# Graph layers on one core: first-stage transfers on other queues, carry index from rows on chip, ninth parts turned two by two

## What is computed

```python
h = relu(layer_norm(x))
# layer 0, per edge and head
score = exp(clip(sum(k[src] * q[dst]) / 8, -5, 5))
wv = segment_sum(v[src] * score, dst) / (segment_sum(score, dst) + 1)
g = h @ Wf + bf + wv @ Wo + bo
x = x + g + layer_norm(g) * gamma + beta
h = relu(layer_norm(x))
# layer 1, per edge; sh: 9 numbers per edge
k = mlp2(edge, k_w1, ...) * sum_s(sh[:, s] * (h[src] @ Cqk[:, s, :]))
v = mlp2(edge, v_w1, ...) * sum_s(sh[:, s] * (h[src] @ Cv[:, s, :]))
alpha = segment_softmax(sum(q[dst] * k), dst)
return x + batch_norm(h @ Wself + segment_sum(v * alpha, dst) @ Wout)
```

## Time and profile before

| | us |
|---|---|
| Median of 3 runs | 3783.44 (3783.2 to 3785.74) |
| Profiled execution: its own time | 3787.59 |
| Profiled execution: span, first to last instruction | 3785.8 |
| First stage, to 182 us | 182 |
| Edge stage of layer 0, to 1254 us | 1072 |
| Between the edge stages, to 1428 us | 174 |
| Edge stage of layer 1, to 3650 us | 2222 |
| Closing stage | 136 |

### The profile page before, as it was taken

The page is one execution under the profiler, slowest core; times in us unless marked ns, Lnnn a source line. Parts: engine busy times, 40 slices in busy tenths (PEclk is TensorE's granted clock), DMA queues, the critical chain, the costliest instruction groups (busy, mean ns, idle before and its releaser), DMA issues. The chain is left out here.

```text
span 3785.8 us, 86852 instructions
## 1 busy us (share of the span) xinstructions
PE 3367.5 (89%) x26344; PEld 3215.3 (85%) x26344; DVE 2836.6 (75%) x4894; ACT 1252.2 (33%) x3131; POOL 1977.1 (52%) x2000
## 2 busy tenths in 40 slices
PE   2099999999999327999999999999999999999963
PEld 1088888888888227999999999999999999999953
DVE  4266666666666227899999999999999989999953
ACT  1033333333333113333333334333333433333320
POOL 3377777777777335544444444444444444444430
PEclk8599999999999658999999999999999999999975
DMA  6499999999999213444444444444444444444420
GB/s 232 164 264 280 279 279 279 280 281 279 278 280 277 85 46 102 122 127 129 126 122 129 129 122 125 130 127 122 128 129 123 125 130 128 121 128 130 123 83 31
DMA packets 845629, 622.17 MB, mean 164 GB/s; under 512 B 492271, under 2 KB 734643, under 8 KB 845292
## 3 DMA queue, kind: packets, MB, share of 16 engines
q1 hardware_dynamic: 681454, 502.39, 43.9%
q0 software_dynamic: 56640, 87.65, 9.8%
q10 hardware_dynamic: 107478, 31.50, 3.7%
HBM read 335.87 MB, written 286.31 MB: 164 GB/s over the span
## 5 line engine op out<-in xcount | busy, mean ns | idle before, releaser
L1410 ACT ACTIVATE z_hi<-bank 128x512 fp32r<-128x512 f32 (+1 forms) x1010 | 559.2, 595 | 1095.8 <-PE bank L1341 1095.7
L803 POOL DMA_INDIRECT kv<-kv_tab,src_i x808 | 762.4, 944 | 284.8 <-issue 189.1
L1315 POOL DMA_INDIRECT xg<-h_tab,src_i x808 | 785.7, 972 | 221.6 <-issue 188.6
L1325 POOL TENSOR_TENSOR kq<-kvs,q_of 128x512 f32<-128x512 f32 x202 | 259.7, 1286 | 951.3 <-DVE kvs L1487 951.3
L1366 PE MATMUL bank<-C_hi,z_hi 128*128 128x256 f32 x4040 | 679.5, 299 | 0.0
L1477 DVE TENSOR_TENSOR z_lo<-bank,z_hi 128x512 fp32r<-128x512 f32 x808 | 520.9, 686 | 190.6 <-ACT z_hi L1410 190.0
L1366 PE MATMUL bank<-C_lo,z_hi 128*128 128x256 f32 x4040 | 609.7, 281 | 0.0
L1341 PE MATMUL bank<-ident,z 128*128 128x128 f32 x4040 | 542.4, 273 | 62.4 <-DVE z L1462 62.4
L1462 DVE TENSOR_TENSOR z<-xg,sh 128x1152 f32<-128x1152 f32 x404 | 549.5, 1360 | 9.2 <-DMA xg<-h_tab,src_i 9.2
L1366 PEld LDWEIGHTS bank<-C_hi,z_hi 128*128 128x128 f32 x4040 | 534.7, 190 | 1.1
L1366 PEld LDWEIGHTS bank<-C_lo,z_hi 128*128 128x128 f32 x4040 | 533.3, 188 | 0.0
(11 more groups left out here) (242 smaller groups left out, 4386.4 us busy)
## 6 DMA issues: line engine op xcount, KB each, us to landing
w_tab<-wsb SPq DMA_DIRECT2D x202, 512.0 KB, 3.4
win<-w_tab SPq DMA_DIRECT2D x202, 512.0 KB, 3.5
sum_edge<-rowt SPq DMA_DIRECT2D x202, 288.0 KB, 2.5
q_edge<-zq SPq DMA_DIRECT2D x202, 256.0 KB
qs<-q_edge SPq DMA_DIRECT2D x202, 256.0 KB, 2.8
sum_edge<-rows ACTq DMA_DIRECT2D x202, 136.0 KB
qs<-q_edge SPq DMA_DIRECT2D x202, 128.0 KB
drow<-dst_tab SPq DMA_DIRECT2D x202, 128.0 KB, 3.2
```

The lines of the kernel that those rows point to most:

```text
L803: pool.indirect_dma_start(kv[b][:, q, :], None, kv0_tab, bass.IndirectOffsetOnAxis(ap=src_i[:, i * Q + q:i * Q + q + 1], axis=0))\
L1315: pool.indirect_dma_start(xg[b][:, q, :], None, h1_tab, bass.IndirectOffsetOnAxis(ap=src_i[:, i * Q + q:i * Q + q + 1], axis=0))\
L1325: pool.tensor_tensor(kq[:, :].rearrange("p (q o) -> p q o", q=Q), kvs[b][:, :, 0:O1], q_of[b % 2][:, :].rearrange("p (q o) -> p q o", q=Q) ...
L1410: nc.scalar.activation(z_hi[b % 2][f, k, :], bank[ZB[k]][f, :], ACT.Copy).then_inc(hi_out, 1)
```

## The change

In the first block SyncE issues the four fills after its three loads, and ACT the pads, the two `near` loads, and then all 31 weights, 25 of which stood in the third block. In the third block SyncE's queue holds the 28 fills and, after them, the first queries; ACT issues the rows first, the two table pads after its copies of `lastrow`, and after its last copy of `kvq` the node tables, the 16-bit list and the mask. The side loads are gone: DVE makes the carry index for 808 tiles on one partition from the turned rows `dst_e` and `lastrow`, PE turns it by seven transposes, DVE copies it. Between the edge stages POOL's scatter waits for the group of four tiles that it needs next. In the edge stage of layer 1, z keeps eight parts a tile; the ninth parts of four tiles lie together in `z_last`, made by one DVE instruction, and PE turns two tiles' ninth parts as one, so the fifth part is two transposes; ACT's copy and DVE's remainder of it become two instructions each, of 64 partitions and two tiles.

```diff
-        sp.wait_ge(pad_set, 4)
...
+        sp.wait_ge(pad_set, 1)
+        for k in range(4):
+            sp.dma_start(*fills[k]).then_inc(filled[k], 16)
 
     @block.scalar
     def _(act):
-        act.wait_ge(pad_set, 1)
-        for k in range(4):
-            act.dma_start(*fills[k]).then_inc(filled[k], 16)
+        act.wait_ge(pad_set, 3)
+        act.dma_start(dst_flat[E:EP + P].unsqueeze(0), padi[:, :]).then_inc(lin, 16)
+        act.dma_start(src_flat[E:EP].unsqueeze(0), zrow[0:1, :, :].bitcast(I32).rearrange(
+            "p a d -> p (a d)")[:, 0:EP - E]).then_inc(lin, 16)
+        act.wait_ge(lin, 64)
+        for n in range(2):
+            act.dma_start(near[:, n, :], dst_flat[n:n + P * NTE].rearrange("(p e) -> p e", p=P))\
+               .then_inc(near_in, 16)
         act.wait_ge(w2z, 3)
         for a, b in loads0:
             act.dma_start(a, b).then_inc(w0_in, 16)
+        for a, b in loads:
+            act.dma_start(a, b).then_inc(W_SEM, 16)
...
         for k in range(4, len(fills)):
             sp.wait_ge(filled[k % 4], 16 * (k // 4))
             sp.dma_start(*fills[k]).then_inc(filled[k % 4], 16)
-            if k == 7:
-                for a, b in loads:
-                    sp.dma_start(a, b).then_inc(W_SEM, 16)
-                for g in range(7):
-                    n = P if g < 6 else NT - 6 * P
-                    lo = 1 if g == 0 else 0
-                    sp.dma_start(before_r[lo:n, g, :], dst_tab[g * P + lo - 1:g * P + n - 1, P - 1:P],
-                                 allow_slow_non_contiguous=True).then_inc(sides_in, 16)
-                    sp.dma_start(after_r[0:n, g, :], dst_tab[g * P + 1:g * P + n + 1, 0:1],
-                                 allow_slow_non_contiguous=True).then_inc(sides_in, 16)
-                sp.wait_ge(dst16_set, 2)
...
-            if k == FILL_BEFORE:
-                sp.wait_ge(proj_out, len(pj_groups))
...
         sp.wait_ge(tabs, 64)
 
         sp.wait_ge(first_got, 16 * 7)
...
-        sp.wait_ge(mask_set, 2)
...
         sp.wait_ge(first_put, 16 * 7)
         sp.wait_ge(dst16_out, 32)
         sp.wait_ge(mask_out, 32)
...
+        for rows, tab in ((dst_r, dst_tab), (src_r, src_tab)):
+            act.dma_start(rows[:, 0:6, :], tab[0:6 * P, :].rearrange("(g t) p -> t g p", g=6))\
+               .then_inc(rows_in, 16)
+            act.dma_start(rows[0:NT - 6 * P, 6, :], tab[6 * P:NT, :]).then_inc(rows_in, 16)
...
+        act.dma_start(q0_tab[N:N + 1, :], zrow[0:1, 0, :]).then_inc(tabs, 16)
+        act.dma_start(q1_tab[N:N + 1, :], zrow[0:1, 0:2, :].rearrange("p a d -> p (a d)")).then_inc(tabs, 16)
...
+        act.wait_ge(proj_out, len(pj_groups))
+        act.dma_start(kv0_tab.rearrange("(p j) d -> p j d", j=NJ), kvq[:, :, 0:2 * D]).then_inc(tabs, 16)
+        act.dma_start(q0_tab[0:N, :].rearrange("(p j) d -> p j d", j=NJ), kvq[:, :, 2 * D:3 * D]).then_inc(tabs, 16)
...
+        act.wait_ge(dst16_set, 2)
...
+        act.wait_ge(mask_set, 2)
...
+        first, final = dst_e[0:1, :], lastrow[0:1, :]
+        step(dve.memset(into[:, 0, 0:1], 0.0))
+        step(dve.tensor_tensor(into[:, 0, 1:], final[:, 0:NTR - 1], first[:, 1:NTR], ALU.is_equal))
+        step(dve.tensor_tensor(into[:, 1, :], first[:, 1:NTR + 1], first[:, 0:NTR], ALU.not_equal))
+        step(dve.tensor_tensor(into[:, 0, :], into[:, 0, :], into[:, 1, :], ALU.mult))
+        step(dve.tensor_scalar(into[:, 0, :], into[:, 0, :], -4.0 * N, 4.0 * N, ALU.mult, ALU.add))
+        dve.tensor_tensor(into[:, 2, :], into[:, 0, :], first[:, 0:NTR], ALU.add).then_inc(into_ready, 1)
...
+        dve.wait_ge(into_mm, 1)
+        step(dve.tensor_copy(into_i[:, 0:6], bank[0][:, 0:6]))
+        step(dve.tensor_copy(into_i[0:NTR - 6 * P, 6:7], bank[0][0:NTR - 6 * P, 6:7]))
...
+        pe.wait_ge(into_ready, 1)
+        for g in range(7):
+            n = P if g < 6 else NTR - 6 * P
+            ins = nc.tensor.transpose(bank[0][0:n, g:g + 1], into[0:1, 2, g * P:g * P + n], ident[0:1, 0:1])
+        ins.then_inc(into_mm, 1)
...
-        pool.wait_ge(q_out, len(groups4))
         for j in range(NJ):
+            if j % 4 == 0:
+                pool.wait_ge(q_out, j // 4 + 1)
...
-z = [sb(f"z{b}", [P, Q, S * D], F32, ph) for b in range(2)]
+z = [sb(f"z{b}", [P, Q, (S - 1) * D], F32, ph) for b in range(2)]
+z_last = [sb(f"z_last{b}", [P, Q * D], F32, ph) for b in range(2)]
...
+def of_half(rows_ap, r):
+    return rows_ap.rearrange("p (h r e) -> p h r e", r=2, e=P)[:, :, r, :]
...
-                for q in range(Q):
-                    ins = nc.tensor.transpose(bank[ZB[k]][:, q * P:(q + 1) * P],
-                                              z[b % 2][:, q, COLS[k]], ident[:, :])
+                turned = [z[b % 2][:, q, k * P:(k + 1) * P] for q in range(Q)] if k < 4 else \
+                    [z_last[b % 2][:, 2 * h * D:2 * (h + 1) * D] for h in range(Q // 2)]
+                for q, part in enumerate(turned):
+                    ins = nc.tensor.transpose(bank[ZB[k]][:, q * P:(q + 1) * P], part, ident[:, :])
...
-                f = slice(D, 2 * D) if k == 4 else slice(0, P)
-                nc.scalar.activation(z_hi[b % 2][f, k, :], bank[ZB[k]][f, :], ACT.Copy).then_inc(hi_out, 1)
+                if k < 4:
+                    nc.scalar.activation(z_hi[b % 2][:, k, :], bank[ZB[k]][:, :], ACT.Copy).then_inc(hi_out, 1)
+                    return
+                for r in range(2):
+                    f = slice(r * D, (r + 1) * D)
+                    ins = nc.scalar.activation(of_half(z_hi[b % 2][f, 4, :], r),
+                                               bank[ZB[4]][f, 0:2 * P].rearrange("p (h e) -> p h e", e=P), ACT.Copy)
+                ins.then_inc(hi_out, 1)
...
+                if half == 0:
+                    dve.tensor_tensor(z_last[b % 2][:, :].rearrange("p (q d) -> p q d", d=D), xg[b][:, :, :],
+                                      sh[b][:, :, S - 1:S].broadcast_to([P, Q, D]), ALU.mult)
                 dve.tensor_tensor(z[b % 2][:, tiles, :].rearrange("p q (s d) -> p q s d", d=D),
-                                  bcast(xg[b][:, tiles, :], 2, S), bcast(sh[b][:, tiles, :], 3, D),
+                                  bcast(xg[b][:, tiles, :], 2, S - 1), bcast(sh[b][:, tiles, 0:S - 1], 3, D),
...
-                    dve.tensor_tensor(z_hi[b % 2][0:D, 4, :], bank[ZB[4]][D:2 * D, :],
-                                      z_hi[b % 2][D:2 * D, 4, :].bitcast(F32), ALU.subtract).then_inc(lo_out, 1)
+                    for r in range(2):
+                        f, g = slice(r * D, (r + 1) * D), slice((1 - r) * D, (2 - r) * D)
+                        ins = dve.tensor_tensor(of_half(z_hi[b % 2][g, 4, :], r),
+                                                bank[ZB[4]][f, 0:2 * P].rearrange("p (h e) -> p h e", e=P),
+                                                of_half(z_hi[b % 2][f, 4, :], r).bitcast(F32), ALU.subtract)
+                    ins.then_inc(lo_out, 1)
```

More of the change, by code:

```diff
@@ L258, in gnn @@
             q0_fill = q0_edge.rearrange("(a p n) d -> a p n d", p=P, n=101)
-            FILL_BEFORE = 17
             fill_parts = [(0, 26), (26, 51), (51, 76), (76, 101)]
@@ L521, in _ @@
                 def _(sp):
[L522 to L525, removed]
                     for k in range(4, len(fills)):
@@ L593, in _ @@
                                              bank[6 + g % 2][0:NP, 0:(b - a) * 3 * D], ACT.Copy).then_inc(proj_out, 1)
+                    act.wait_ge(proj_out, len(pj_groups))
+                    act.dma_start(kv0_tab.rearrange("(p j) d -> p j d", j=NJ), kvq[:, :, 0:2 * D]).then_inc(tabs, 16)
+                    act.dma_start(q0_tab[0:N, :].rearrange("(p j) d -> p j d", j=NJ), kvq[:, :, 2 * D:3 * D]).then_inc(tabs, 16)
+                    act.wait_ge(dst16_set, 2)
+                    act.dma_start(dst16_tab[0:6 * P, :].rearrange("(g t) p -> t g p", g=6), dst16_r[:, 0:6, :])\
+                       .then_inc(dst16_out, 16)
+                    act.dma_start(dst16_tab[6 * P:NT, :], dst16_r[0:NT - 6 * P, 6, :]).then_inc(dst16_out, 16)
+                    act.wait_ge(mask_set, 2)
+                    act.dma_start(mask_tab[0:6 * P, :].rearrange("(g t) p -> t g p", g=6), mask_r[:, 0:6, :])\
+                       .then_inc(mask_out, 16)
+                    act.dma_start(mask_tab[6 * P:NT, :], mask_r[0:NT - 6 * P, 6, :]).then_inc(mask_out, 16)
                     act.wait_ge(W_SEM, n_weights)
@@ L670, in _ @@
                     step(dve.tensor_tensor(over[:, :], tf[:, 0, :], has[:, :], ALU.mult))
-                    dve.wait_ge(sides_in, 16 * 14)
-                    for n, g0, g1 in ((P, 0, 6), (NT - 6 * P, 6, 7)):
-                        at = (slice(0, n), slice(g0, g1))
-                        step(dve.tensor_tensor(into[0:n, 0, g0:g1], before_r[0:n, g0:g1, 0], first_i[at], ALU.is_equal))
-                        step(dve.tensor_tensor(into[0:n, 1, g0:g1], after_r[0:n, g0:g1, 0], first_i[at], ALU.not_equal))
```

(10 more changed lines are left out.)

28 lines of the change are left out of this document (2 added, 26 removed).

## The result

| | before | after |
|---|---|---|
| median of 4 runs, us | 3783.37 (3783.2 to 3785.74) | 3731.97 (3729.88 to 3734.77) |
| ratio, 95% interval | | 0.9863 (0.9846 to 0.988) |
| profiled execution / its span, us | 3787.59 / 3785.8 | 3729.88 / 3728.2 |

The change gains 51.4 us by the medians and 57.6 us by the two profiled spans. The forecast was 66.2 us.

The account below looks back on a forecast made before the run. PE was taken to bound the second edge stage, with DVE 0.93 us a step behind; gains of 44 + 7.2 + 15 = 66.2 us gave 3717.2 us off the median, forecast range 3700 to 3725 us (chance 0.65).

Parts of the forecast that it names:

- term 2: Between the edge stages: query scatter starts 0.83 us after ACT's first group instead of its last, 7.2 us gained.
- rival (a): First stage: queues alone change nothing, the barrier behind ACT's issues eats the gain; 51 us gained, 3732 us; chance 0.18.
- Term 1: Second edge stage: two transposes instead of four save PE 0.22 us a step over 202 steps, 44 us.
- Nothing else on PE changes: Edge step: apart from the fewer transposes PE's work stays the same, with its 56 matmuls.
- (b): Edge stage: DVE becomes the bound through costly short instructions; 14 to 22 us left of 44, 3739 to 3747 us; chance 0.08.
- (c): Edge stage: DVE's added instructions cost over 1.04 us a step, so the kernel gets slower, 3852 us; chance 0.03.
- (d): Edge stage: two transposes take four's time as PE waits for DVE's bank release; gain 22 us, 3761 us; chance 0.03.
- Term 3: First stage: queue holes close, so the last fill comes at 126 us against 141.80, 15 us gained.
- I take 9.5: First stage: the rows' loads beside fills take 9.5 us, between 5.9 and 32.
- adds up: First stage: the tables' 25 us, on few engines, add to the fills' 65 us after 36 us, making 126 us.
- tables are served last: First stage, a bound: the tables come after the fills and seven gathers of 1.3 us each follow; 7 us gained.
- the middle value: First stage: last fill at 126 us, 15 us gained, chosen between bounds of -6 and 26 to 32 us.

Follow-up runs that it names:

- run 5: Changed kernel with one more product of the ninth parts' size on DVE in each edge step, into an unread buffer: 3730.8 us in one run.
- run 6: Changed kernel with two more products of the ninth parts' size on DVE in each edge step: 3736.2 us in one run.
- run 2: Kernel before with only the query scatter's change, waiting for each group of four tiles: 3780.65 us, ratio 0.9989.
- run 7: Changed kernel with SyncE's third-block fills held until the rows of the edge lists have landed: 3735.3 us, ratio 0.9869.
- run 3: Kernel before with only the first stage's part, queues and carry index from rows on chip: 3774.15 us, ratio 0.997.
- run 8: Changed kernel with the queries' table written ahead of keys and values, and the gathers waiting for it alone: 3727.2 us, ratio 0.9847.
- run 10: Changed kernel with each node table's write cut into 112 and 13 partitions: 3725.32 us, ratio 0.984.
- run 11: Changed kernel with fills held for the rows, weight loads behind the tables, queries' table first, tables cut in two: 3711.1 us, ratio 0.9807.
- run 4: Changed kernel with the ninth parts' two transposes each made twice, so PE has its old 20 a step: 3767.5 us in one run.

## Why the prediction was right or wrong

**In sum:** the sign and the range held, the mechanisms of the first two terms were the right ones, and the third had one wrong order in it, but 3717 us was 14.8 us too low, outside the forecast's own 3700 to 3725. Of that, 8.6 us are terms of the sum (by spans 57.6 instead of 66.2: -7.2 edge stage, -3.0 first stage, +2.1 between the edge stages, -0.5 elsewhere; the +2.1 are luck, see term 2), and 6.2 us are the profiled executions' places among their runs. The time is that of rival (a), 3732 us, whose account was wrong, for it gave the first stage nothing (that the tables come last, with the gathers behind them, it had right): a right number is no proof of a cause.

**Term 1, the ninth parts: mechanism right, size off.** The group of two costs the 0.22 us of the working, DVE's first wait closed, and the second kept 0.55 us where 0.4 was expected. DVE's pieces were priced well: 1.22 us for z instead of 1.36, 0.42 for the new product, 0.43 for each half remainder against 0.41. The failed step is "Nothing else on PE changes": the other rows took 0.04 us more, most of it in the products, so a step lost 0.18 us instead of 0.22, 36 us instead of 44. The 10.62 us of the working were also 0.02 too low from the start: its one step of 10.84 us stands for a mean of 10.857. Rivals (b) and (c) fall with runs 5 and 6, for even 0.68 us more on DVE leave the step as it is; (d) falls with the 0.22 us.

**Term 2, the scatter: right.** The scatter started 0.84 us after the first group's end, 7.2 us earlier in the trace and, against its own first group, in run 2. ACT's first group in the changed kernel, whose scatter is the mark of 1359.75:

```profile
1358.31 0.60 ACT L1181 ACTIVATE q1n<-bank 125x512 f32<-125x512 f32 x1 [1.29 <-PE bank L1153]
```

The stretch gained 2.1 us more, but ahead of the scatter: PE's products there ran at a mean granted clock of 0.70 instead of 0.63 over 12 us (1.0 and 0.5 are its levels of 2.4 and 1.2 GHz). The third column from the end is the clock's; before:

```profile
1316.00:1328.00 12.00, 11.60 (x67) 11.60 (x67) 0.00 (x0) 1.75 (x6) 0.00 (x0) 0.63 0.01 1
```

After:

```profile
1304.00:1316.00 12.00, 11.70 (x75) 11.70 (x76) 0.00 (x0) 1.78 (x6) 0.00 (x0) 0.70 0.00 1
```

The clock fell later in the work, after 4.4 us of these products instead of 2.6. No edit touches this code, and from stage three's start to ACT's first group it took 118.46 us in the kernel before, 116.30 in the changed kernel and 119.45 in run 6, whose code up to there is the changed kernel's. So the 2.1 us are luck, and run 2 has the scatter's 7.2 us without them.

**Term 3, the first stage: size near, steps wrong in opposite directions.**
- The block began at 32.44 us instead of 36: ACT's 31 issues took 18.4 us (11.95 to 30.36), not 22.
- "I take 9.5" for the rows failed: 20.5 us beside fills, within the bound of 32, whose mechanism (each row waits for one piece of a fill) is what the packets show. Run 7 shows the fills as the cause: 5.5 us without them.
- That the tables' time "adds up" on those engines held as a sum and failed as an order. Fills from 32.4 to 95 us and tables from there to 121 end 5 us ahead of the 126 of the working. But the working let the scatter follow the last fill; the tables were served last, moving almost nothing beside the fills, and the seven gathers' 10.5 us came behind them. That was the bound "tables are served last", and the middle value was the wrong choice.
- So the scatter started at 131.62, between the 126 of the forecast and the 135 of that bound, or at the bound less the 3.6 us by which the block began earlier: 10.2 us gained. The stage's tail gave 1.8 us more (from scatter to next stage 38.0 us instead of 39.9): before, SyncE wrote the mask behind qfirst's rows, from 177.93 to 178.90 us, and now ACT issues it at 133.35. The working had counted that write's move at nothing. By run 3's trace the same stage gains 9.0 us instead of 12.0, so the first stage's share of the 51 us also holds some luck.

The Trainium skill has rival (a) as a rule: a second issuing engine saves only issue time (DMA: Bandwidth & Descriptors, "Issuing engines are not separate DMA queues"). Here issue time was large, 19.94 us for one write, and with the fills alone in one queue the share was 0.99 from 31 to 95 us. That run 3's 7 to 16 us came from the order within a queue, and not from the second issuing engine, is argued from these rows; no run has the new order on one engine.

## What to carry to other kernels

When a queue is split, ask what each transfer will now stand beside. A transfer in small packets that is issued into a stretch saturated by large ones may end after them, as the tables did here: price it at both ends, and look for who waits for it. Where several chains end within 10 us of one another, an edit of one stops at the next chain, as runs 8 and 10 did, so price the next chain before the edit. Trace the same code more than once before a mark is trusted to a microsecond. The wait that a trace shows on an engine can understate its room (run 6: 0.55 us shown, 0.68 us of work fitted).

## What the runs showed of the hardware

- Row loads, 5.4 to 5.9 us alone (runs 11 and 7), took 20.5 us beside fills that saturate the DMA engines. The queues took turns by packets, 540 of the rows' to 536 of the fills', at 0.5 KB to 5.7.
- The table writes took 25.4 us behind the fills before and 26 us in the changed kernel; from issue to readiness 32.1 us (81.29 to 113.39) and 38.2 us. The fills beside them lost nothing that can be seen: 63 us for 28, where the working had 65.
- Behind the fills the table writes from 125 partitions show a DMA share of 0.38 before and 0.41 in the changed kernel, those in pieces of 112 and 13 partitions 0.92 (run 10), with a few gathers beside them.
- ACT was held for 25.98 us by the issue of one table write (82.86), as SyncE was for 19.94 us before; in run 7 the corresponding issue took 39.7 us.
- The 56 products of an edge step took 7.00 instead of 6.97 us in the mean when four transposes became two, at the same granted clock of 0.99 over the stage; with the transposes back (run 4) they took 6.97 again.
